# Row sums of a masked softmax: pairs of probability tiles added on GpSimd, TensorE summing every fourth tile

## The reference, cut to what matters

```python
Wh = h @ W                                   # 2048 x 64
e = leaky_relu(u[:, None] + v[None, :], 0.2) # 2048 x 2048
att = softmax(where(adj > 0, e, -9e15), axis=1)
h = elu(att @ Wh)
```

## Time and profile before

| | |
|---|---|
| median of 3 runs | 730.22 us |
| lowest to highest | 729.61 to 732.3 us |
| the profiled execution, device time | 733.23 us |
| span in its profile | 731.4 us |
| PE busy | 586.5 us (80%) |
| DVE busy | 381.8 us (52%) |
| ACT busy | 255.8 us (35%) |
| POOL busy | 33.4 us (5%) |
| first to last exponential of the four GAT layers | 76.3 to 480.7 us |

### The profile page before, as it was taken

The page is one execution under the profiler, slowest core; times in us unless marked ns, Lnnn a source line. Parts: engine busy times, 40 slices in busy tenths (PEclk is TensorE's granted clock), DMA queues, the critical chain, the costliest instruction groups (busy, mean ns, idle before and its releaser), DMA issues.

```text
span 731.4 us, 7417 instructions
## 1 busy us (share of the span) xinstructions
PE 586.5 (80%) x3106; PEld 205.2 (28%) x3140; DVE 381.8 (52%) x524; ACT 255.8 (35%) x257; POOL 33.4 (5%) x29
## 2 busy tenths in 40 slices
PE   5532889966789966699966889996686799999997
PEld 4300113324112324222233113245222222233332
DVE  1744667623666633576733667624898567730001
ACT  1586445330545530455531545321100354400000
POOL 1300000201000100110000000012000000000000
PEclk9555899986899985899986899996799799999999
DMA  7393000000000000000000000000000000000000
GB/s 301 123 408 159 1 0 1 1 0 1 1 0 1 1 1 0 1 1 1 0 1 1 0 1 1 0 1 1 0 1 0 1 0 1 0 1 1 0 1 29
DMA packets 3040, 19.08 MB, mean 26 GB/s; under 512 B 320, under 2 KB 320, under 8 KB 960
## 3 DMA queue, kind: packets, MB, share of 16 engines
q1 hardware_dynamic: 2864, 17.83, 6.0%
q10 hardware_dynamic: 144, 0.79, 0.3%
HBM read 18.09 MB, written 0.52 MB: 25 GB/s over the span
## 4 chain that ended last, share of the span: by engine, by line
PE 63%; DVE 22%; ACT 5%; issue 5%; DMA 4%; POOLq 0%; POOL 0%; DVEq 0%; ACTq 0%
PE PROD L544 12%; PE PROD L749 8%; PE S L554 8%; PE X L749 7%; PE X L536 7%; DVE aB L1114 4%; DVE X L918 4%; DMA big<-in_adjT 3%; PE X L710 3%; PE X L713 3%; PE M L522 2%; ACT big L335 2%; DVE aB L910 1%; DVE big L909 1%; DVE nadj L1029 1%
## 5 line engine op out<-in xcount | busy, mean ns | idle before, releaser
L918 DVE SCALAR_TENSOR_TENSOR X<-wB,v,aB 128x1024 f32<-128x1024 f32 x128 | 161.6, 1291 | 86.0 <-ACT big L335 85.1
L335 ACT ACTIVATE big<-X,v 128x1024 f32<-128x1024 f32 x128 | 137.4, 1111 | 146.6 <-PE X L536 146.2
L544 PE MATMUL PROD<-big,Wh 128*64 128x512 f32 x512 | 133.5, 640 | 4.8 <-ACT big L335 4.6
L536 PE MATMUL X<-nadj,bigI 128*128 128x512 bf16 x230 | 67.8, 395 | 41.2 <-DVE X L918 37.6
L554 PE MATMUL S<-big,onesf 128*32 128x512 f32 x512 | 68.3, 605 | 0.0
L544 PEld LDWEIGHTS PROD<-big,Wh 128*64 128x64 f32 x512 | 31.2, 142 | 86.1 <-ACT big L335 58.9
L522 PE MATMUL M<-big,level 128*32 128x512 fp8e4 x256 | 27.0, 552 | 33.2 <-ACT big L368 23.6
L710 PE MATMUL X<-nadj,bigI 128*128 128x512 bf16 x120 | 39.7, 408 | 13.3 <-DVE aB L1114 8.7
L536 PEld LDWEIGHTS X<-nadj,bigI 128*128 128x128 bf16 x256 | 16.3, 98 | 114.9 <-DVE X L918 73.2
L1114 DVE TENSOR_TENSOR aB<-aB,X 128x1024 f32<-128x1024 f32 x32 | 39.1, 1221 | 4.5 <-PE X L713 3.5
L713 PE MATMUL X<-wB 96*128 96x512 bf16 (+1 forms) x128 | 40.8, 401 | 0.0
(11 more groups left out here) (243 smaller groups left out, 551.0 us busy)
## 6 DMA issues: line engine op xcount, KB each, us to landing
big<-in_adjT SPq DMA_DIRECT2D x16, 1024.0 KB, 8.7
cst<-in_cst ACTq DMA_DIRECT2D x1, 771.5 KB, 5.2
x<-in_xT SPq DMA_DIRECT2D x1, 512.0 KB, 5.9
out<-x SPq DMA_DIRECT2D x2, 256.0 KB, 2.0
```

Source lines behind the costliest of these rows:

```text
L335: act.activation(prob[:, t % U, :], X[t % 2][:], ACT.Exp, bias=v2[l % 2][:, k:k + 1]).then_inc(p_ready, 1)
L536: last = pe.matmul(X[t % 2][:, hh * BANK:(hh + 1) * BANK], bigI[:], nadj[:, k, half_cols(c, hh)], start=False, stop=True, skip_group_check ...
L544: pe.matmul(PROD[c][feat(hh), :], Wh[l % 2][:, k, :], prob[:, t % U, hh * BANK:(hh + 1) * BANK], start=k == 0, stop=k == NB - 1)
L918: dve.scalar_tensor_tensor(X[t % 2][:], wB[:, cols(c)], v8[l % 2][:, k:k + 1], aB[:, cols(c)], ALU.max, ALU.add).then_inc(x_written, 1)
```

## The change

GpSimd gets a new step, `pair_sums`: as soon as both tiles of a pair have their exponentials (`p_ready`), it adds the two 128x1024 float32 tiles of `prob` into one of two buffers `psum2[p % 2]` (another part of `big`) and signals `pair_ready`. TensorE's `sums` now runs once for two pairs, on the two buffers of `psum2`, with the same four strips, and signals `pair_free`, which gives both `psum2` buffers back to GpSimd. ScalarE now waits, before it writes a `prob` buffer, for two semaphores: `p_used` (TensorE's products of the old pair are done) and `pair_ready` (GpSimd has added it). The last sums of a chunk come behind the first pair of the next chunk, or behind the loop; `total` and `reciprocal_rows` of chunk 0 come one pair later, and the places of ScalarE's and VectorE's steps in chunk 1 move by one or two tiles. GpSimd's older steps stand at fixed places between the pair sums.

```diff
--- before
+++ after
+        psum2 = big[:, 5 * N:7 * N].bitcast(f32).rearrange("p (u n) -> p u n", u=2)
...
@@ -282,6 +285,15 @@
                 pool.tensor_scalar(hq[:, c, :], h0[:, c, :], SLOPE, None, ALU.mult).then_inc(hq_ready, 1)
                 pool.tensor_scalar(xq[:, c, :], h0[:, c, :], SLOPE, -(1 - SLOPE), ALU.mult, ALU.add).then_inc(xq_ready, 1)
 
+            def pair_sums(l, c, pairs):
+                for p in pairs:
+                    n = (NCH * l + c) * NB // 2 + p
+                    pool.wait_ge(p_ready, 2 * n + 2)
+                    if n >= 2:
+                        pool.wait_ge(pair_free, n // 2)
+                    pool.tensor_tensor(psum2[:, p % 2, :], prob[:, 2 * n % U, :], prob[:, (2 * n + 1) % U, :],
+                                       ALU.add).then_inc(pair_ready, 1)
+
             def part_of(t, c):
                 return t[:, CB * c:CB * (c + 1)]
 
@@ -289,14 +301,27 @@
                 inverse_root(part_of(rr, c), part_of(var, c))
             for c in range(NCH):
                 below_one(c)
-            for lf in (1, 2):
-                for c in range(NCH):
-                    inverse_root(part_of(rr, c), part_of(var, c))
-                    if lf == 1:
-                        pool.wait_ge(x_new, c + 1)
-                        below_one(c)
-            for c in range(NCH):
-                mix_terms(c)
+            for l in range(GAT):
+                if l == 2:
+                    mix_terms(0)
+                    pair_sums(l, 0, range(6))
+                    mix_terms(1)
+                    pair_sums(l, 0, range(6, 8))
+                else:
+                    pair_sums(l, 0, range(NB // 2))
+                pair_sums(l, 1, range(5))
+                if l == 0:
+                    pool.wait_ge(x_new, 1)
+                    below_one(0)
+                pair_sums(l, 1, range(5, 6))
+                if l < 2:
+                    inverse_root(part_of(rr, 0), part_of(var, 0))
+                pair_sums(l, 1, range(6, 8))
+                if l < 2:
+                    inverse_root(part_of(rr, 1), part_of(var, 1))
+                if l == 0:
+                    pool.wait_ge(x_new, 2)
+                    below_one(1)
             for c in range(NCH):
                 inverse_root(part_of(rr, c), part_of(var, c))
                 inverse_root(part_of(ff, c), part_of(var, c))
@@ -331,11 +356,12 @@
                 t = NB * (NCH * l + c) + k
                 act.wait_ge(x_masked, t + 1)
                 if t >= U:
-                    act.wait_ge(p_free, (t - U) // 2 + 1)
+                    act.wait_ge(p_used, (t - U) // 2 + 1)
+                    act.wait_ge(pair_ready, (t - U) // 2 + 1)
                 act.activation(prob[:, t % U, :], X[t % 2][:], ACT.Exp, bias=v2[l % 2][:, k:k + 1]).then_inc(p_ready, 1)
 
             def sum_copy(l, c):
-                act.wait_ge(p_free, (NCH * l + c + 1) * NB // 2)
+                act.wait_ge(pair_free, (NCH * l + c + 1) * NB // 4)
                 act.activation(sS[:], S[:], ACT.Copy).then_inc(s_copied, 1)
                 act.activation(pS[:], PROD[c][:], ACT.Copy).then_inc(p_copied, 1)
 
@@ -378,9 +404,9 @@
                         w_broadcast(2 * l + 1)
                 for k in range(NB):
                     exponential(l, 1, k)
-                    if k == 1:
+                    if k == 3:
                         sum_copy(l, 0)
-                    if k == 5:
+                    if k == 7:
                         elu_exp(l, 0)
                     if k == 9 and l < 2:
                         square(2 * l + 2)
@@ -541,19 +567,22 @@
                 t = NB * (NCH * l + c) + k
                 pe.wait_ge(p_ready, t + 1)
                 for hh in range(2):
-                    pe.matmul(PROD[c][feat(hh), :], Wh[l % 2][:, k, :], prob[:, t % U, hh * BANK:(hh + 1) * BANK],
-                              start=k == 0, stop=k == NB - 1)
+                    last = pe.matmul(PROD[c][feat(hh), :], Wh[l % 2][:, k, :], prob[:, t % U, hh * BANK:(hh + 1) * BANK],
+                                     start=k == 0, stop=k == NB - 1)
+                if k % 2:
+                    last.then_inc(p_used, 1)
 
             def sums(l, c, k):
 
                 t = NB * (NCH * l + c) + k
-                if k == 1 and t > 1:
+                if k == 3 and t > 3:
                     pe.wait_ge(s_copied, NCH * l + c)
+                pe.wait_ge(pair_ready, (t + 1) // 2)
                 for strip in range(4):
-                    tile, hh = t - 1 + strip // 2, strip % 2
+                    pair, hh = strip // 2, strip % 2
                     last = pe.matmul(S[32 * strip:32 * strip + 32, :], onesf[:, 0:32],
-                                     prob[:, tile % U, hh * BANK:(hh + 1) * BANK], start=k == 1, stop=k == NB - 1)
-                last.then_inc(p_free, 1)
+                                     psum2[:, pair, hh * BANK:(hh + 1) * BANK], start=k == 3, stop=k == NB - 1)
+                last.then_inc(pair_free, 1)
 
             def total(l, c):
 
@@ -649,16 +678,19 @@
                         elif c == 0:
                             mask(l, 1, 0)
                             mask(l, 1, 1)
-                        sums(l, c, k + 1)
+                        if c and p == 0:
+                            sums(l, 0, NB - 1)
+                        elif p % 2 == 0 and p:
+                            sums(l, c, k - 1)
                         if c == 0:
                             if p == 0 and l:
                                 w_broadcast(2 * l + 1)
                             if p == 2 and l == 2:
                                 root_broadcast(1)
                             continue
-                        if p == 0:
+                        if p == 1:
                             total(l, 0)
-                        if p == 1:
+                        if p == 2:
                             reciprocal_rows(l, 0)
                         if l < 2:
                             if p == 3:
@@ -685,6 +717,7 @@
                                 centre_again(0)
                             if p == 7:
                                 keys(0)
+                sums(l, 1, NB - 1)
                 total(l, 1)
                 reciprocal_rows(l, 1)
                 if l < 2:
@@ -1053,11 +1086,11 @@
                         input_rows(1)
                 for k in range(NB):
                     exponents(l, 1, k)
-                    if k == 4:
+                    if k == 5:
                         reciprocals(l, 0)
-                    if k == 6:
+                    if k == 7:
                         normalised(l, 0)
-                    if k == 7:
+                    if k == 8:
                         activated(l, 0)
                     if l < 2:
                         if k == 10:
```

More of the change, by code:

```diff
@@ L191, in program @@
         p_ready = sem("p_ready")
-        p_free = sem("p_free")
+        p_used = sem("p_used")
+        pair_ready = sem("pair_ready")
+        pair_free = sem("pair_free")
         s_copied = sem("s_copied")
```

## The result

The changed kernel takes 842.02 us (median of 4 runs, 836.03 to 843.15) against 730.22: 1.151 times as long, 95% interval 1.145 to 1.157. The direction was forecast, the size was not: 112 us against 31, outside the range of 724 to 804.

What follows compares the result with a forecast made beforehand. Engines were taken to wait for each other in turn, with bare pairs of 3.83 us. Terms -14 + 17 + 6 + 11 + 7 + 2 + 2 = +31 us took 733.2 to 764, less 3: 761 us, range 724 to 804.

Steps and rivals of the forecast that it cites:

- a removed sum is worth 0.1 us in a bare pair: TensorE, chunk 0: each removed sum saves 0.1 us, not 1.0; with chunk 1's savings, -14 us together.
- the hole behind the masks: TensorE in a bare pair: the 1.0 us sums fill time it would idle anyway, awaiting the first exponential.
- I take four times the faster, 2.8 us: GpSimd's pair add: length taken as four times the faster one-input operation of 0.70 us, so 2.8 us.
- 4 x 0.28 = 1.1 us: VectorE's second tile write: each GpSimd add delays it 1.1 us, scaled from 0.28 us lost beside a smaller read.
- Rival 1: The whole add blocks VectorE, 1.2 us a pair in chunk 0, 0.8 in chunk 1: +58, 788 us; chance 22%.
- In chunk 1 TensorE's steps cover most of it; I take 0.2 for 28 pairs, +6 us: Chunk 1: VectorE's delay from the adds is mostly covered, leaving 0.2 us a pair, +6 us.
- The bare pairs, 0.6 us for the hold and 0.4 for the buffers: Chunk 0, 28 pairs: 0.6 us each from delayed tile writes (+17), 0.4 from late psum2 buffers (+11).
- The two buffers, +11 us: psum2 is freed only every second pair, so ScalarE waits for late adds: 0.4 us for each of 28, +11 us.
- The end of a layer ... +1.8 us: Last exponential to copy: sums wait for the 2.8 us add while products run beside it; +1.8 us, four times, +7.
- ScalarE's and VectorE's moved places cost nothing: Later places of ScalarE's and VectorE's steps add 0 us: they follow `total`, and one pair of cover remains.
- Rival 4: The clock falls in the loop as waits stretch pairs to 5 to 6 us: +25, 786 us; chance 5%.
- the +2 us for the clock: TensorE's longer gaps make another stretch at the lower, 1.2 GHz clock level likely: +2 us.

Runs made afterwards that it cites:

- e1: Changed kernel with VectorE's tile write reading its first tensor from PSUM (one SBUF input) and ending in min: 784.11 us, ratio 1.0698.
- e5: Kernel before with the sums of every second pair left out and nothing in their place: 722.13 us, ratio 0.9855.
- e7: Kernel before with every second pair's sums left out and TensorE alternating products and masks tile by tile: 708.65 us, ratio 0.9695.
- e3: Changed kernel with each pair sum replaced by two memsets of the same buffer, so GpSimd reads nothing; all waits kept: 742.92 us, ratio 1.0134.
- e8: Changed kernel with three psum2 buffers in place of two: 818.55 us, ratio 1.1184.
- e9: Changed kernel with three psum2 buffers and VectorE's tile write with one SBUF input: 755.46 us, ratio 1.0317.
- e13: Kernel before with half the sums and only the changed kernel's moved places of steps, GpSimd as before: 753.22 us, ratio 1.0270.
- e4: Kernel before with all its sums, plus 64 GpSimd adds of constant tiles that nobody waits for: 799.94 us, ratio 1.0927.

## Why the prediction was wrong in size

By its own steps. First, where the time went: each pair is measured from its first exponential to the next pair's, and the distances are summed over the four layers (us, one profile of each kernel).

| stretch | before | changed | e1 |
|---|---|---|---|
| 28 pairs of chunk 0, without `target_rows` | 115.7 | 139.3 | 116.7 |
| 4 pairs with `target_rows` (pair 4) | 27.4 | 44.6 | 43.5 |
| chunk 1, pairs 8 to 14 | 135.4 | 180.8 | 147.7 |
| pair 15 to the next layer, three times | 122.5 | 139.7 | 136.1 |
| ahead of layer 0's pair 0, and from layer 3's pair 15 on | 330.4 | 335.1 | 335.9 |

- **"a removed sum is worth 0.1 us in a bare pair", saving 14 us**: right in kind, e5 gives 8.9. The reason given, the hole behind the masks, is borne out by e7.
- **"I take four times the faster, 2.8 us"**: alone the add takes 2.35 us (the shortest 2.34). The Trainium skill's table (GPSIMD Engine Reference, Performance versus the Vector engine) was nearer: an estimate of 2.25 from its 4497 ns.
- **"4 x 0.28 = 1.1 us"**, what an add costs VectorE: the first of two steps that failed. The measured hold is 2.13 us (3.42 - 1.29). I had scaled the 0.28 us by which L910 was late. But GpSimd was itself held behind L909 there, and how much of its operation was still reading when L910 came, the rows do not say, and no run settled it; a delay that may come from the tail of an overlap alone cannot be scaled. The other half of the evidence, GpSimd standing until VectorE was done, was read correctly and set aside. Rival 1, to which I gave 22%, is the mechanism: e1, e3 and the 3.42 us show it. The Trainium skill (SBUF — State Buffer, Who interferes with whom) has the two exclude each other for the whole instruction, and an instruction that only writes SBUF not taking part; the runs agree, with 2.13 of 2.35 us held and 1294 ns beside the memsets.
- **"In chunk 1 TensorE's steps cover most of it; I take 0.2 for 28 pairs, +6 us"**: the second step that failed, and the larger in time. From e1 to the changed kernel, where only the tile write's second operand differs, chunk 1 grows by 33.1 us, 1.2 a pair, while its 64 tile writes take 36 us longer (mean 1859 ns against 1289): hardly anything there covers the holds, and the lower clock (below) adds its part. All in all chunk 1 grew by 45.4 us, where saving and holds together were forecast at -6.
- **The bare pairs, 0.6 us for the hold and 0.4 for the buffers**: two pairs grew by 2.11 us (9.77 - 2 x 3.83), 1.06 a pair, and the 28 pairs of chunk 0 by 23.6 us, against 17 + 11 - 2 = 26. That this came out is luck. Buffers and saving together add 1.0 us there (before to e1) and the tile write's operand 22.6, 0.8 a pair; and of the 3.97 us of holds in two pairs (2.13 + 1.84) 1.86 were absorbed, where I had 2 x 0.5. Why so much is absorbed stays open.
- **Rival 1's own price, +58 us**, was short by half, but not in the bare pairs, for which it had 1.2 us each. Not every other pair escapes: the two `psum2` buffers put two adds back to back, and each holds one write. What it missed is chunk 1, as above, and that `target_rows` and `activated` read two SBUF tensors as well; the two instructions of `target_rows` take 17 us more in the groups (L942 and L943, 2298 and 2271 ns instead of 1222 and 1261, 8 each), and the four pairs with them 17.2.
- **The two buffers, +11 us**: e8 and e9 give 23.5 and 28.7, and not where I had put them. Two buffers hurt where VectorE has other work, in pairs 4 and 12 (21.6 of the 29.9 us between the profiles of e1 and e9), and hardly in a bare pair.
- **"The end of a layer ... +1.8 us"**: 1.4 us in layer 0 (4.70 against 3.28). The stretch from pair 15 to the next layer grew by 17.2 us in three layers all the same; in layer 0, 5.3 of its 7.6 lie in pair 15 itself, whose two exponentials start 9.5 us apart instead of 4.3.
- **"ScalarE's and VectorE's moved places cost nothing"**: wrong. Against e5, pairs 11 and 12 of e3 take 3.0 to 4.7 us more in a layer, 17 us in all, of which pair 9 returns 1 a layer (3.9 instead of 4.9): 13 of the 21 us between e3 and e5 (18 between their profiles). How much of it is the places and how much the later sums stays open, since e13 has a wait of its own.
- **Rival 4 and the +2 us for the clock**: the granted clock of the whole profile, 0.859 against 0.871, hides a change. Between the first and last exponential of a layer it is 0.89, 0.84, 0.86 and 0.82 in the changed kernel against 0.96, 0.95, 0.97 and 0.97 before; the time at the lower level there adds up to 117 us against 23. The two stretches below are pairs 8 to 10 of layers 0 and 1, the same work in both, in 14.7 us at the full level and in 18.5 where it fell (length, then busy us of PE, PEld, DVE, ACT, POOL, granted clock):

```profile
122.30:137.10 14.80, 11.17 (x52) 3.25 (x52) 12.49 (x8) 7.68 (x8) 8.89 (x3) 1.00 0.01 2
260.10:278.60 18.50, 15.39 (x53) 4.96 (x54) 12.51 (x8) 7.54 (x8) 9.61 (x3) 0.73 0.00 0
```

So the clock has a share in the 112 us, which was not separated; in e3, without the reads, the layers have 0.94 to 0.96 again. The bulk does not need it: e4 loses its 67 us at 0.94 to 0.98, with products as short as before (mean 640 ns before, 726 in the changed kernel, 638 in e4; the groups of the last two):

```profile
L570 PE MATMUL PROD<-big,Wh 128*64 128x512 f32 x512 | 155.3, 726 | 6.1 <-ACT big L361 5.9
```

```profile
L568 PE MATMUL PROD<-big,Wh 128*64 128x512 f32 x512 | 132.8, 638 | 4.8 <-ACT big L359 4.6
```

So from 730: the sums give back 9, the rebuilt waits and places take 21 (742.9 in e3 against 722.1 in e5), and the reads, with the lower clock behind them, take 99, of which 58 go with the tile write's second operand alone.

## What to carry to other kernels

Before work goes to an idle GpSimd, look at the operands of VectorE's instructions, not at the busy share: with two SBUF inputs on VectorE's side, a GpSimd instruction that reads SBUF stops it for nearly its whole length, and the wait hides in VectorE's own duration. Add the two engines' times for such pairs and compare the sum with the period of the loop; here 2 x 1.29 + 2.13 = 4.71 us is more than 3.83, and a bare pair took 4.9. And a removed instruction is worth what the next wait on its engine leaves of it, which the order of the remaining work can change (8.9 us in one order, 29.7 in the other, of 34 removed).

## What the runs showed of the hardware that I had not expected

- A GpSimd add of two 128x1024 float32 tiles takes 2.35 us and holds a two-input VectorE instruction for 2.13 of them, even one that starts 0.02 us behind it; a VectorE instruction under way holds the add in the same manner (3.34 us).
- A cut instruction lets the other engine in between, but 256 columns take 1109 ns with the waits and 713 at the shortest, against 2342 for 1024: an estimate from the two shortest is 0.17 us fixed and 2.1 ns a column.
- Alternating products and masks on TensorE costs about 0.27 us in a pair (4.10 against 3.83) although the matmuls are the same.
- In the layers of the changed kernel, with longer waits and half the sums, the granted clock was 0.82 to 0.89 against 0.95 to 0.97, where the mean of the whole profile hardly moved (0.859 against 0.871).
